# Perceiver cross-attention kernel on Trainium2: the side work of TensorE, VectorE and ScalarE laid out anew from one table per engine, the output projection in two halves

## What is computed

```python
x = x + xattn(ctx_1024, layernorm(x), ...)   # 16 heads of 64, keys and values from context and latents
x = x + attn(layernorm(x), ...)              # differential attention over the 64 latents
x = x + ffn(layernorm(x), ...)               # 8 experts, top 2
# xattn, per batch:
q = l @ Wq; k, v = split(concat([x, l]) @ Wkv)
w = softmax((q * scale) @ (k * scale).T)
out = (w @ v).reshape(64, 1024) @ Wo
```

## Time and profile before

| | |
|---|---|
| median of three runs | 988.33 us |
| profiled execution | 989.81 us |
| its span | 988.1 us |
| TensorE, busy | 920.4 us (93%) |
| VectorE | 786.7 us (80%) |
| ScalarE | 704.7 us (71%) |
| GpSimd | 377.1 us (38%) |

### The profile page before, as it was taken

How to read it: one execution, slowest core, us unless ns; L and a number is a source line. 1 busy time by engine, 2 the same in 40 slices (tenths; PEclk the granted TensorE clock), 3 DMA queues, 4 the chain that set the end, 5 groups by cost and what they waited for, 6 DMA issues and landing times.

```text
span 988.1 us, 20490 instructions
## 1 busy us (share of the span) xinstructions
PE 920.4 (93%) x8246; PEld 494.5 (50%) x8246; DVE 786.7 (80%) x1591; ACT 704.7 (71%) x1003; POOL 377.1 (38%) x376
## 2 busy tenths in 40 slices
PE   7569999999999999999999999999999999979975
PEld 5344445454545454545454545454545454557742
DVE  5968898888787878797979797878786866668965
ACT  4566878787878787878787878787878667535631
POOL 6562034242524242424243425242424132253243
PEclk9799999999999999999999999999999999979987
DMA  6202031303030212120212121212122100000000
GB/s 206 68 17 64 4 88 12 80 12 81 12 79 16 77 17 75 18 74 19 74 19 74 20 72 19 74 24 68 24 56 29 29 1 23 1 23 23 2 6 16
DMA packets 74565, 41.95 MB, mean 42 GB/s; under 512 B 62276, under 2 KB 69864, under 8 KB 74472
## 3 DMA queue, kind: packets, MB, share of 16 engines
q1 hardware_dynamic: 74184, 39.60, 16.9%
q10 hardware_dynamic: 288, 1.05, 0.3%
HBM read 25.98 MB, written 0.59 MB: 27 GB/s over the span
## 4 chain that ended last, share of the span: by engine, by line
PE 66%; DVE 21%; ACT 5%; issue 4%; DMA 1%; POOL 1%; SPq 0%; POOLq 0%; ACTq 0%; DVEq 0%
PE S L2086 8%; PE S L2077 8%; PE S L2080 8%; PE OA L2110 7%; PE OA L2113 7%; PE OA L2116 7%; PE WW L2023 7%; DVE mx L1469 6%; DVE region L1481 4%; DVE region L1460 2%; ACT region L1791 2%; PE WW L2050 1%; PE WW L2051 1%; PE WW L2052 1%; DVE amx L764 1%
## 5 line engine op out<-in xcount | busy, mean ns | idle before, releaser
L1791 ACT ACTIVATE region<-S,sigma 128x1024 f16<-128x1024 f32 x208 | 231.9, 1115 | 155.5 <-PE S L2086 154.4
L1481 DVE TENSOR_TENSOR region<-S,region 128x1024 f16<-128x1024 f32 x208 | 252.5, 1214 | 72.6 <-ACT S L1795 72.6
L1469 DVE TENSOR_REDUCE mx<-WW 128x1 f32<-128x512 f32 (+1 forms) x480 | 259.8, 584 | 34.2 <-PE WW L2023 28.4
L1795 ACT ACTIVATE S<-S,sigma 128x1024 f32<-128x1024 f32 x208 | 225.3, 1083 | 0.0
L2077 PE MATMUL S<-region,xT 128*128 128x512 f16 (+1 forms) x416 | 124.2, 380 | 4.2 <-DVE region L1481 3.3
L2023 PE MATMUL WW<-xT,region 128*128 128x512 f16 x360 | 122.2, 381 | 4.1 <-DVE mx L1469 2.5
L2110 PE MATMUL OA<-region,xk 128*128 128x512 f16 (+1 forms) x416 | 124.2, 380 | 0.0
L2086 PE MATMUL S<-region,xT 128*128 128x512 f16 (+1 forms) x416 | 124.2, 380 | 0.0
L2113 PE MATMUL OA<-region,xk 128*128 128x512 f16 (+1 forms) x416 | 124.1, 380 | 0.0
L2116 PE MATMUL OA<-region,xk 128*128 128x512 f16 (+1 forms) x416 | 123.9, 379 | 0.0
L2080 PE MATMUL S<-region,xT 128*128 128x512 f16 (+1 forms) x416 | 123.7, 379 | 0.0
(11 more groups left out here) (315 smaller groups left out, 1800.6 us busy)
## 6 DMA issues: line engine op xcount, KB each, us to landing
raw<-ctx SPq DMA_DIRECT2D x16, 768.0 KB
rb<-inv_dram SPq DMA_DIRECT2D x16, 512.0 KB, 3.7
xT<-xk SPq DMA_TRANSPOSE x48, 3.3
left_row<-left_pT SPq DMA_DIRECT2D x48, 2.0 KB
raw<-ctx SPq DMA_DIRECT2D x16, 32.5 KB
WO_lo<-L_xattn_Wq ACTq DMA_DIRECT2D x1, 512.0 KB, 3.8
WO_hi<-L_xattn_Wkv ACTq DMA_DIRECT2D x1, 512.0 KB, 4.7
lx<-x SPq DMA_DIRECT2D x1, 512.0 KB, 8.3
```

The source lines that it names most:

```text
L1469: nc.vector.tensor_reduce(mx[:, r, c:c + 1], W[BANK[("m", n)]][:, 0:width], AX.X, ALU.max)\
L1481: nc.vector.tensor_tensor(p_lo[k], src, p_hi[k], ALU.subtract).then_inc(lo_done.sem, 1)
L1791: nc.scalar.activation(p_hi[k], src, ACT.Exp, scale=sigma[:, 0:1])
L1795: nc.scalar.activation(src, src, ACT.Exp, scale=sigma[:, 0:1]).then_inc(e_done.sem, 1)
```

## The change

The common plan and the constants give way to three tables: `TENSOR` (a pair of lists for each unit, early and late), `VECTOR` (one list for each unit, in which "low" marks the low part), `SCALAR` (three lists for each unit: before the high exponential, between the two, behind the full one). The names "lf" and "lt" become "left_scores" and "left_turned". The weighings `("weigh", 12)` and `("weigh", 11)` and the leftover's (`("left", 0)`, now in unit 9 between m20 and m21) become items. The projection becomes `("pj", 0)` and `("pj", 1)`, eight heads each, in the same bank.

```diff
-PLAN = [([], []),
-        ([], [("pj", 0)]),
-        ([("lf", 0)], []),
-        ([("q", 0), ("q", 1)], some(0, 2)),
-        (some(2, 2), some(4, 2)),
-        ([("lt", 0), ("q", 2), ("q", 3)], some(6, 1)),
-        (some(7, 2), some(9, 2)),
-        (some(11, 2), some(13, 2)),
-        (some(15, 2), some(17, 2)),
-        (some(19, 2), some(21, 2)),
-        (some(23, 2), some(25, 2)),
-        (some(27, 2), some(29, 3)),
-        ([("mt", 0), ("mt", 1)], [])]
-LATENTS_AT = 0
+TENSOR = [([], [("weigh", 12)]),
+        ([("left_scores", 0), ("q", 0), ("pj", 0)], []),
+        ([("pj", 1), ("q", 1)], some(0, 1)),
+        (some(1, 1), some(2, 2)),
+        (some(4, 1), some(5, 1)),
+        ([("left_turned", 0), ("q", 2), ("q", 3)], some(6, 1)),
         (some(7, 2), some(9, 2)),
-        (some(11, 2), some(13, 2)),
-        (some(15, 2), some(17, 2)),
-        (some(19, 2), some(21, 2)),
+        (some(11, 2), some(13, 1)),
+        (some(14, 2), some(16, 2)),
+        (some(18, 2), some(20, 1) + [("left", 0)] + some(21, 2)),
         (some(23, 2), some(25, 2)),
         (some(27, 2), some(29, 3)),
-        ([("mt", 0), ("mt", 1)], [])]
-LATENTS_AT = 0
+        ([("mt", 0), ("mt", 1)], [("weigh", 11)])]
+
+VECTOR = [("stat", "stat", "stat", "stat", "latents", "stat", "left_sum", "low", ("split", 0), ("split", 1), "stat", ("q", 0), ("split", 2), "stat",),
+          ("low",),
+          ("stat", "stat", "low", "stat", "left_low", ("split", 3), ("q", 1), ("m", 0), ("m", 1), "stat", ("m", 2), "stat", ("m", 3), "stat",),
+          ("low", ("m", 4), ("m", 5),),
+          ("combine", "low", ("q", 2), ("q", 3), ("m", 6),),
+          ("low", ("m", 7), ("m", 8), "inverse", ("m", 9), ("m", 10),),
+          ("low", ("m", 11), ("m", 12), ("m", 13),),
+          ("low",),
+          (("m", 14), ("m", 15), ("m", 16), ("m", 17), "low", ("m", 18), ("m", 19), ("m", 20), ("m", 21), ("m", 22),),
+          ("low",),
+          (("m", 23), ("m", 24), ("m", 25), ("m", 26), "low", ("m", 27), ("m", 28), ("m", 29), ("m", 30), ("m", 31),),
+          ("low",),
+          ("low",)]
+
+SCALAR = [([], [], ["outputs"]),
+          ([], [], [("q", 0)]),
+          ([], [], ["projected", "left_exp", ("q", 1)]),
+          ([], [], []),
+          ([], [], []),
+          (["left_copy"], [("q", 2), ("q", 3)], []),
+          ([], [("norm", 0)], []),
+          ([("norm", 1)], [], [("norm", 2)]),
+          ([], [("norm", 3)], [("norm", 4)]),
+          ([("high", 0)], [("norm", 5)], []),
+          ([], [("norm", 6)], [("norm", 7)]),
+          ([("high", 1)], [("norm", 8), ("norm", 9)], [("norm", 10)]),
+          ([("norm", 11), ("norm", 12)], [], [("shift", 0), ("shift", 1)])]
+LEFT_AT = 9
...
-STATS_AT = {0: range(0, 4), 1: range(4, 7), 2: range(7, 11), 3: range(11, 13)}
-COMBINE_AT = 5
-NORMALISE_AT = {6: [0], 7: [1, 2, 3], 8: [4, 5, 6], 9: [7, 8, 9], 10: [10, 11], 11: [12]}
-RECIPROCALS_AT = 6
-OUTPUTS_HIGH_AT = {10: 0, 11: 1}
-LEFT_EXP_AT, LEFT_LOW_AT, LEFT_AT = 3, 4, 10
...
-        X1_AT, H_AT, TILE0_AT, KEYS1_AT, VALUES1_AT = 2, 8, 9, 10, 11
+        X1_AT, H_AT, TILE0_AT, KEYS1_AT, VALUES1_AT = 3, 8, 9, 10, 11
...
             def side_item(item, turn):
                 kind, k = item
                 w, p = side_out(item, turn), turn.off % 2
-                bank_free(item, turn)
+                if item != ("pj", 1):
+                    bank_free(item, turn)
...
                 if kind == "pj":
                     pe.wait_ge(o_split.sem, o_split.upto(turn, 1))
-                    for n in range(2 * H):
+                    for n in range(H * k, H * k + H):
...
-                ins.then_inc(pe_item[kind].sem, 1)
+                if item != ("pj", 0):
+                    ins.then_inc(pe_item[kind].sem, 1)
...
                 for u in range(UNITS):
                     scores(b, u)
-                    side_items(PLAN[u][0])
+                    side_items(TENSOR[u][0])
                     if b is LAST and u == LAT:
                         wait(pe, "kx", Turn(1))
                         side_item(("pj", 0), old)
+                        side_item(("pj", 1), old)
                     if u >= 2:
                         weigh(b, u - 2)
-                    if u == LATENTS_AT and post:
-                        weigh(old, LAT)
-                    if u == LEFT_AT:
-                        weigh_left(b)
-                    if u == LAT and b is not LAST:
-                        weigh(b, LAT - 1)
-                    side_items(PLAN[u][1])
+                    side_items(TENSOR[u][1])
```

The engines' loops take the items from their tables in the order written; an item of another turn is left out where that turn doesn't exist, as before. ScalarE's loop:

```diff
+                    before, between, behind = SCALAR[u]
...
+                    side_items(b, before, prep, post, stats)
                     exponentials_high(b, u)
...
+                    side_items(b, between, prep, post, stats)
                     exponentials_full(b, u)
...
+                    side_items(b, behind, prep, post, stats)
```

More of the change, by code:

```diff
@@ L105, in bank_of_items @@
+LEFT_AT = 9
 def bank_of_items():
     order = []
-    for u, (early, late) in enumerate(PLAN):
-        order += early + ([("ol", 0), ("ol", 1)] if u == LATENTS_AT else []) + late
-    return {item: n % 2 for n, item in enumerate(order)}
+    for early, late in TENSOR:
+        for item in early + late:
+            if item == ("weigh", 12):
+                order += [("ol", 0), ("ol", 1)]
+            elif item[0] not in ("weigh", "left") and item != ("pj", 1):
+                order.append(item)
+    banks = {item: n % 2 for n, item in enumerate(order)}
+    banks[("pj", 1)] = banks[("pj", 0)]
+    return banks
@@ L1380, in _ @@
             stats_combine(128, TB, link, scale=1.0 + EPS, eps=EPS * EPS).then_inc(var_rdy.sem, 1)
-            for u in range(COMBINE_AT + 1):
-                statistics(Turn(0), u)
+            for t in range(TILES):
+                statistic(Turn(0), t)
+            combine(Turn(0))
             dve.wait_ge(rstd_rdy.sem, 1)
@@ L1399, in statistics_next @@
                     ins.then_inc(dve_step.sem, 1)
-                    statistics(Turn(1), COMBINE_AT)
+                    combine(Turn(1))
             def amax_map(k):
@@ L1818, in projected, with side_items @@
                   .then_inc(free["pj"].sem, 1)
[L1820 to L1827 removed]
+            def side_items(b, items, prep, post, stats):
+                for item in items:
+                    if item == "outputs" and post:
+                        outputs(b.plus(-1))
+                    if item == "projected" and b.off > 1:
+                        projected(b.plus(-2))
+                    if item == "left_exp":
+                        left_exponentials(b)
+                    if item == "left_copy":
+                        left_copied(act, nc.scalar.copy, b)
+                    if item[0] == "q" and prep:
+                        queries_high(b.plus(1), item[1])
+                    if item[0] == "shift" and prep:
+                        shift_row(b.plus(1), item[1])
+                    if item[0] == "high" and post:
+                        outputs_high(b.plus(-1), item[1])
+                    if item[0] == "norm" and stats:
+                        normalise(b.plus(2), [item[1]])
             def slot(b, prep=True, post=True, stats=True):
[L1830 removed]
+                old = b.plus(-1)
                 for u in range(UNITS):
[L1832 removed]
+                    before, between, behind = SCALAR[u]
                     if b.off == 0 and u == 3:
@@ L2130, in side_items @@
                     for item in items:
-                        if item[0] in OWN:
+                        if item == ("weigh", LAT):
+                            if post:
+                                weigh(old, LAT)
+                        elif item == ("weigh", LAT - 1):
+                            if b is not LAST:
+                                weigh(b, LAT - 1)
+                        elif item[0] == "left":
+                            weigh_left(b)
+                        elif item[0] in OWN:
                             side_item(item, b)
```

133 lines of the change are left out of this document (57 added, 76 removed).

## The result

The changed kernel took 982.14 us (median of nine runs, 978.46 to 986.03) against 990.26 us of the kernel before beside it: ratio 0.9925, 95% interval 0.9909 to 0.9941, faster by 0.75%. The forecast was 972.5 us, range 965 to 982: right in its direction, twice too large in its size. The ratio leaves out one disturbed run of the kernel before, of 1202.84 us. The changed kernel, unaltered, was measured twice more, beside the experiments: 0.988 [0.9863, 0.9897] and 0.9904 [0.9886, 0.9922]. About 1% is the fair figure of three sessions.

The account below looks back on a forecast made before the run. TensorE was taken as the bound. Turn 0 -1.7, turn 1 -0.5, turns 2 to 13 -14.4, turn 14 -1.4, LAST +2.3 sum to -15.7 us: 974.1 profiled, 972.5 against the median, range 965 to 982.

Parts of the forecast that it names:

- The bound: TensorE, busy 93% of the span; no matmul is removed, so at most some 1.8 us per repeated turn.
- the 0.72 us wait: Unit 5, before query item 3: gone once ScalarE's copy of the turned leftover weights precedes the high exponential.
- half a projection covers low(0): Unit 2: scores(2) start unhindered at 6.6 us; without that cover TensorE waits from 5.2 to 6.1.
- the new waits at m26, m30 and m31: Late units of a turn: new TensorE waits of 0.14, 0.17 and 0.14 us in the bank rotation.
- the shift rows: Unit 12: rows moved behind the full exponential finish at 47.9, TensorE ready at 47.8, a 0.16 us wait.
- rival 3: VectorE's `inverse` between m8 and m9 blocks if denominators land late: slower, about 998 us; chance 0.07.
- LAST: Loses 2.3 us: waits net +0.3, and three early normalisations held by GpSimd's products, 3.8 us instead of 1.8.
- low(1) at 8.4, ended 9.7: Units 0 to 2: VectorE's low part ends before scores(3) need it at 11.5 us; cost nothing.
- comes to some 47.1: Turn 1, without a projection to cover the wait for low(0): from 47.65 to some 47.1 us, -0.5.
- My -1.7: Turn 0: gap before scores(2) filled, clock gain taken as 0.6 us, later waits gone; together -1.7, bounds -1.1 and -2.3.
- All fit, two of them narrowly; cost zero: DMA and GpSimd queues of a turn: first product half ready at 32.76 us, high(0) wants it at 32.84.
- rival 2: Output halves ahead of high(9) and high(11) delay ScalarE if products end late: 0.6 us a turn, 980 us; chance 0.20.

Follow-up runs that it names:

- experiments 4: Kernel before with only the copy of the turned leftover weights moved ahead of the high exponential of unit 5: 980.29 us, ratio 0.9909.
- experiment 7: Changed kernel with the projection undivided, both halves behind the scores of unit 2: 989.44 us, ratio 0.9998 to the kernel before.
- the first control: Changed kernel, unaltered, measured a second time: 977.75 us, ratio 0.988 to the kernel before.
- experiment 2: Changed kernel with split 2 moved on VectorE from the end of unit 0 to behind low(1): 977.58 us, ratio 0.9894 to the kernel before.
- experiment 5: Changed kernel with ScalarE's copy of the turned leftover weights put back behind the high exponential of unit 5: 989.02 us, ratio 0.9997 to the kernel before.
- the controls: Changed kernel, unaltered, measured twice more: 977.75 and 980.96 us, ratios 0.988 and 0.9904 to the kernel before.
- experiment 3: Changed kernel with ScalarE's first output half behind the two exponentials of unit 9: 977.13 us, ratio 0.9896 to the kernel before.
- Experiment 8: Changed kernel with both projection halves ahead of the scores of unit 2: 991.55 us, ratio 1.0022 to the kernel before.

## Why the prediction was off

**Right.** The bound; that the 0.72 us wait goes with the copy (experiments 4 and 5: 0.70 and 0.73 us a turn, the largest single part of the gain); that half a projection covers low(0) in unit 2 (experiment 7; without it I had said ready at 5.2, wait until 6.1, and it waits 0.85 us); the new waits at m26, m30 and m31, 0.18, 0.15 and 0.19 us by starts where I had 0.14, 0.17 and 0.14; the shift rows, 0.21 for my 0.16; that no wait stands ahead of turn 14's projection; rival 3's place never blocked. Turn 14 came within 0.2 us. In LAST the waits alone came out in the first control, where all three normalisations met products and the clock stayed at 2.4 GHz: +2.3, as forecast. Its two parts were each off by 0.4, the other way round: the three begin 2.1 us later than before and not 1.7, and take 3.4 us and not 3.8:

```profile
816.34 3.42 DVE L657 TENSOR_SCALAR raw<-raw,sm 128x128 f32<-128x128 f32 x3
```

The port rule of the Trainium skill (SBUF — State Buffer, Terms), that the pair is locked for a whole instruction and the loser blocks, fits both in the main: the tiles and the cast are held until GpSimd's instruction ends. They end 0.09 and 0.28 us behind it, though, sooner than the 0.34 and 0.42 us that they take alone.

**The steps that failed**, in us of the profiled execution:

1. *"low(1) at 8.4, ended 9.7"* and *"Cost nothing, covered by 2.8 us of projection"* for units 0 to 2: low(1) starts at 9.18 of the turn. I had used the port rule in LAST, where tiles meet products, and not in the walk, where split 2 had been moved right beside GpSimd's low parts of splits 0 and 1. The cast of 1.39 us, where it takes 0.69 in the kernel before and 0.42 alone, puts a wait of 0.16 ahead of m1 in every repeated turn; that and the shift row make the turn 48.09 for 47.95 to 47.97. Price 1.6 in turns 2 to 13; experiment 2 takes out 0.17 a turn and comes to 47.92.
2. *Turn 1 "comes to some 47.1"*: 48.08. The same cast without a projection in front of it. TensorE waits for low(0), q0's low part and, longest, 1.21 by starts, for q1's:

```profile
126.93 0.39 PE L2058 MATMUL WW<-xT,region 128*128 128x512 f16 x1 [1.05 <-DVE region L1496]
```

   Experiment 2 gives 47.11, my number. Price 0.9. Turn 0 has the same waits, and itself gained only 0.8 us although the clock stayed at 1.00 from 72 to 76 us (0.57), where I had taken only half of that gain. The other 1.0 in the first row of the balance lies ahead of the loop, where the change does nothing: the first high exponential started at 68.2 us in the kernel before and in experiment 5, at 66.2 to 67.2 in the other eleven profiles. My -1.7 was met by luck.
3. *"All fit, two of them narrowly; cost zero"*: the first product half had 0.1 us of margin to the output half, and landings vary by more. Turn 3 gives back 1.0, the controls 1.3 and 1.5 over all turns. This is rival 2's mechanism, in one to three turns instead of in all; experiment 3 takes it away. I had priced it as a shift of every turn, when the thing to price was the spread of a landing against a margin.
4. *LAST*: +3.3 for +2.3. I took three held normalisations and stopped there. In this profile only two were held, which by itself costs less than forecast; but the idle stretch that they make for TensorE was followed by the clock of 1.2 GHz, for which the forecast had no term. Experiment 8, with the same two held and the same 2.73 us, puts the clock's part at 1.7 us. That the longer idleness brings the fall is argued from the thirteen profiles (none of four against four of nine); what decides within the nine stays open.
5. *Behind the turns: zero*: +3.7 in the profile of the result, 0.0 and +0.7 in the controls. This part is no effect of the change. The thirteen profiles show between 137.0 and 141.1 us for it, with the same instructions.

Of the 8.3 us between forecast and result, 3.7 are the fifth step, 2.5 the cast, 1.0 a landing, 1.0 LAST. Without the fifth the profiled execution (982.4 us) would have been at 978.7, inside the range, as both controls' medians are; but still 4.6 us above the 974.1 forecast for it, for the other steps. So that the time came out above the range and not in its upper part goes back to the clock in the late stages, as far as one profile tells; that the forecast gain was too large, in all three sessions, goes back to the first four steps.

## What to carry to other kernels

When a table of side work is laid out anew, hold every cast and every normalisation of VectorE (the two kinds that were held here) against what GpSimd does at that moment, and price it as lasting until the GpSimd instruction that it meets has ended; one entry moved past a neighbour took 14.5 us off VectorE's casts here, and 0.17 us off a turn. Place a consumer on an in-order engine with a margin larger than the spread of the transfers it depends on, and after finding an idle stretch of TensorE ask for the clock behind it. Compare stages and not only totals: two profiles of one and the same kernel differ by 4.5 us here. Before a large new layout, try its best single move alone: here it gave as much as all of it.

## What was not expected of the hardware

A cast of 128x508 elements from f32 to f16 on VectorE took 0.42 us alone and 1.39 us beside GpSimd's elementwise subtraction, and ended 0.28 us behind it. VectorE's low part, which reads PSUM, took 1.20 us right beside the next such subtraction of GpSimd's (both began at 460.7 us), no longer than elsewhere. The small write of reciprocals took 1.4 us to land in nearly every turn and 2.2 to 3.1 us in one and the same turn of every kernel. TensorE's granted clock fell to 0.50 with idle stretches of 2.73 and 3.76 us and stayed at 1.00 with one of 3.39 us in the same place of the same program, and with 2.73 and 3.70 us in two of its variants, so the length of the idle stretch alone does not decide it. The time of the same last stages lay between 137.0 and 141.1 us from one execution to the next.
